# Attention over 32 heads: row maxima run 15 units ahead of the scores, per head instead of per group

## The reference

```python
q = x @ Wq
k = x @ Wk
v = x @ Wv
latent_kv = (k + v) @ W_down_kv
k_rec = latent_kv @ W_up_k
v_rec = latent_kv @ W_up_v
qh, kh, vh = (heads(q), heads(k_rec), heads(v_rec))
scale = 1.0 / (jnp.sqrt(jnp.float32(D_MODEL)) + 1e-08)
scores = jnp.einsum('bhqd,bhkd->bhqk', qh, kh) * scale
scores = jnp.clip(jnp.nan_to_num(scores, nan=-1000000000.0), -CLAMP, CLAMP)
decay = jnp.exp(-LAMBDA_DECAY * TIME_STEP * jnp.abs(idx[:, None] - idx[None, :]))
scores = scores * decay[None, None, :, :]
scores = jnp.clip(jnp.nan_to_num(scores, nan=-1000000000.0), -CLAMP, CLAMP)
attn = jax.nn.softmax(scores, axis=-1)
out = jnp.einsum('bhqk,bhkd->bhqd', attn, vh)
```

## Time and profile before

| | us |
|---|---|
| median of 3 runs | 954.49 |
| lowest, highest | 953.7, 958.48 |
| profiled execution | 959.48 |
| its span | 958.0 |
| attention in it (to the last output of the last group) | about 478 |
| mean granted clock of TensorE | 0.869 |

### The profile page before, as it was taken

One profiled execution on the slowest core, in us unless ns is written; L12 is line 12 of the kernel. 1 busy time (PEld: TensorE's weight loads), 2 busy tenths in 40 slices (PEclk: granted clock), 3 DMA queues, 4 the chain that ended last, 5 costly groups with the idle time before them and its releaser, 6 DMA issues. The chain is left out here.

```text
span 958.0 us, 25373 instructions
## 1 busy us (share of the span) xinstructions
PE 780.9 (82%) x10797; PEld 464.3 (48%) x10797; DVE 605.5 (63%) x1412; ACT 484.0 (51%) x974; POOL 220.0 (23%) x239
## 2 busy tenths in 40 slices
PE   6386999999999999999863958999998696026990
PEld 4012555555555555554442944666664354024770
DVE  3797769788878978780065232767676544762444
ACT  5522778787787778788831543434343222001222
POOL 3983121111121121212203724000000000005631
PEclk9555899999999999999965976999999797556995
DMA  5561215141314121000076126200000002201104
GB/s 190 147 228 61 66 27 76 26 77 30 71 35 72 33 68 38 4 3 5 2 233 175 49 61 227 72 1 1 2 1 1 0 1 67 69 0 39 40 26 143
DMA packets 45747, 59.08 MB, mean 62 GB/s; under 512 B 11924, under 2 KB 22877, under 8 KB 45632
## 3 DMA queue, kind: packets, MB, share of 16 engines
q1 hardware_dynamic: 42512, 51.47, 20.4%
q0 software_dynamic: 2304, 4.74, 1.9%
q10 hardware_dynamic: 816, 1.23, 0.4%
HBM read 42.09 MB, written 15.07 MB: 60 GB/s over the span
## 5 line engine op out<-in xcount | busy, mean ns | idle before, releaser
L800 DVE CUSTOM_DVE_ANT_0 junk<-row,rest 128x1024 bf16<-128x1024 f32 x256 | 307.8, 1223 | 60.4 <-PE row L421 47.1
L649 ACT ACTIVATE prob<-score 128x512 f32<-128x512 f32 x512 | 278.5, 612 | 85.7 <-PE score L421 81.0
L421 PE MATMUL score<-stack 75*32 75x128 bf16 (+3 forms) x3840 | 204.9, 300 | 5.7 <-DMA stack<-neg_rows 1.3
L514 PE MATMUL out_ps<-prob,v_aug 128*32 128x256 f32 x2048 | 153.9, 384 | 1.9 <-ACT prob L649 1.9
L421 PE MATMUL row<-stack 72*32 72x512 bf16 x1792 | 140.6, 389 | 2.1 <-DVE top L800 1.5
L421 PEld LDWEIGHTS score<-stack 75*32 75x32 bf16 x3840 | 91.9, 97 | 95.1 <-ACT prob L649 17.6
L736 POOL TENSOR_SCALAR_AFFINE_SELECT prob<-prob 128x512 f32<-128x512 f32 x64 | 40.6, 634 | 295.7 <-ACT prob L649 295.7
L514 PEld LDWEIGHTS out_ps<-prob,v_aug 128*32 128x32 f32 x2048 | 61.4, 111 | 38.6 <-ACT prob L649 3.3
L421 PEld LDWEIGHTS row<-stack 72*32 72x32 bf16 x1792 | 47.2, 98 | 35.4 <-issue 5.0
L1945 PE MATMUL outs<-vm_w,mixed 128*64 128x256 f32 x512 | 61.7, 381 | 1.8 <-issue 1.8
L1426 PE MATMUL up_ps<-rows_t,up_w 128*128 128x320 f32 (+1 forms) x192 | 60.0, 438 | 1.4 <-DVE rows_t L1638 1.2
(11 more groups left out here) (312 smaller groups left out, 1058.3 us busy)
## 6 DMA issues: line engine op xcount, KB each, us to landing
stack<-parts_dram SPq DMA_DIRECT2D x288, 64.0 KB
parts_dram<-prob SPq DMA_DIRECT2D x12, 256.0 KB, 3.2
parts_dram<-stack SPq DMA_DIRECT2D x12, 256.0 KB, 3.0
results<-x_tok SPq DMA_DIRECT2D x12, 256.0 KB, 3.6
up_w<-in_L_ffn_w_dram SPq DMA_DIRECT2D x1, 2048.0 KB, 9.6
rows<-x_tok SPq DMA_DIRECT2D x8, 256.0 KB, 3.7
y<-results SPq DMA_DIRECT2D x8, 256.0 KB, 4.2
up_w<-in_L_ffn_wg_dram SPq DMA_DIRECT2D x1, 2048.0 KB, 11.3
```

The lines of the kernel that those rows point to most:

```text
L421: last = pe.matmul(out[c:c + 32, :], keys[:, c:c + 32], queries, start=True, stop=True)
L514: last = pe.matmul(out_ps[at:at + 32, part * (S // 4):(part + 1) * (S // 4)], v_aug[g.third][:, tile, h, :], moving[:, 2 * part:2 * part + ...
L649: act.activation(prob[tile % 2][:, h, part * HALF:(part + 1) * HALF], score[n % NS][:, :], ACT.Exp).then_inc(exped, 1)
L800: dve.tensor_tensor_reduce(junk[:, n % 2, :], row[n % 2][:, :], rest[:, S - P - tile * P:2 * S - P - tile * P], 1.0, LOWEST, ALU.mult, ALU ...
```

## The change

What it does, piece by piece:

- **Units by head.** The groups of four are gone from the order. Attention is now 256 steps, one for each head m and key tile t (step = 8m + t). A step has two score units, a late unit at t = 3 and 7 (four diagonal blocks of one head), a row unit of step + LEAD (LEAD = 15), sometimes one extra slot (`slots_at`), and the products of key tile t-2. Row units, transposed maxima, turned outputs and the verdict share the two `row` buffers in one order (`slot_at`, `free_row`).
- **Start.** 15 wide row units run ahead of the first score, instead of 32.
- **Maxima.** They are split on GpSimd, per head, in four dependent operations on 8 columns (`split_top`), transposed by PE NEG_LAG = 2 slots after the head's last row unit, copied by DVE (`copy_neg`), stored by SP, 24 source rows into 3 rows of the stack (`store_neg`). The three keys are now -1 instead of 1 (`TWO_MINUS_ONES`), so nothing is negated.
- **Masks.** One affine select of 128 columns for each step, and one of 512 for each late unit.
- **Loads.** The stacks are now two, with four slots of two heads (a pair) each. The DRAM layout of the parts has the dimension ahead of the head, and one DMA (`load_block`) brings 24 partitions (three parts x 8 dimensions) of 2 heads, 96 KB: on side 0 the three query parts, on side 1 one key part three times. A pair and half takes 6, a pair 12 (`fill`), instead of 36 loads of 64 KB for four heads. SP issues `fill(pair + 3)` after the last score of the preceding pair (36 score units a pair), and behind it the stores of two heads' maxima.
- **Outputs.** A group's outputs are turned by 8 smaller transposes into a `row` buffer; the products of a head that opens a group are delayed so that the copy of the sums can pass.
- **Setup.** The key weights are folded first. The query weights are reordered by DVE. DVE splits both halves of batch 0, GpSimd half 0 of batch 1 in the setup and half 1 of it in the steps 0 to 10 of the pipeline (with ScalarE). ScalarE squares the four projections, and 32 one-column matmuls (`lengths`) ahead of the first wide row unit sum them into squared lengths.
- **Verdict.** The judging of the clamps is done in the last steps of attention, with no branch inside it; if it fails, the general routine does the attention afresh afterwards.

The core of the diff:

```diff
+def load_block(sp, dram, stack, pair, half, side, k, loaded):
+    at, h = k * NPART * HD, 2 * (pair % 2)
+    group = pair // 2
+    if side == 0:
+        rows = dram["parts"][0, half, :, group, :, h:h + 2, :]
+    else:
+        rows = dram["parts"][1, half, k, group, :, h:h + 2, :].unsqueeze(0).to_broadcast([NPART, HD, 2, S])
+    sp.dma_start(stack[at:at + NPART * HD, half, side, h:h + 2, :], rows).then_inc(loaded, 16)
+def load_pair(sp, dram, stack, pair, half, loaded):
+    for side in range(2):
+        for k in range(NPART):
+            load_block(sp, dram, stack, pair, half, side, k, loaded)
+LOADS = 2 * NPART
+LEAD = 15
+NEG_LAG = 2
+VERDICT_AT = 2
+OUT_AT = 4
 def attention(nc, mem, dram, io):
...
+        def leads_group(m):
+            return m > 0 and m % GH == 0
+        def weighs_at(step):
+            m, t = step // SB, step % SB
+            if t < 2:
+                return [("tile", m - 1, SB - 2 + t)] if m else []
+            if leads_group(m):
+                tiles = {4: (0, 1), 5: (2, 3), 6: (4,), 7: (5,)}.get(t, ())
+            else:
+                tiles = (t - 2,)
+            order = [("tile", m, tile) for tile in tiles] if m < NH else []
+            if t == 2 and m:
+                order.append(("late", m - 1, 1))
+            if t == SB - 1 and m < NH:
+                order.append(("late", m, 0))
+            return order
...
+        def slots_at(step):
+            n = step + LEAD
+            if n < NR:
+                yield "row", n
+            m, r = divmod(n - NEG_LAG, SB)
+            if r == SB - 1 and 0 <= m < NH:
+                yield "neg", m
+            if step >= GH * SB and step % (GH * SB) == OUT_AT:
+                yield "out", step // (GH * SB) - 1
+            if step in (STEPS - LEAD + VERDICT_AT, STEPS - LEAD + 2 * VERDICT_AT):
+                yield "verdict", (step - STEPS + LEAD) // VERDICT_AT - 1
+        LAST = STEPS + OUT_AT + 1
...
+            sp.wait_ge(rows_set, 1)
+            for k in range(NPART):
+                store_parts(sp, 0, 0, 0, k, kept[0][k])
+            store_parts(sp, 0, 0, 1, 0, kept[1][0])
+            for k in range(NPART):
+                sp.wait_ge(kept[0][k], 16)
+            for k in range(NPART):
+                load_block(sp, dram, stack[0], 0, 0, 0, k, stacks_in[0][0])
+            for k in range(1, NPART):
+                store_parts(sp, 0, 0, 1, k, kept[1][k])
+            for k in range(NPART):
+                sp.wait_ge(kept[1][k], 16)
+                load_block(sp, dram, stack[0], 0, 0, 1, k, stacks_in[0][0])
+            load_pair(sp, dram, stack[0], 1, 0, stacks_in[0][1])
+            for side in range(2):
+                for k in range(NPART):
+                    store_parts(sp, 0, 1, side, k, stored[0])
+            sp.wait_ge(stored[0], FILL * 16)
+            for pair in range(2):
+                load_pair(sp, dram, stack[0], pair, 1, stacks_in[1][pair])
+            def store_neg(m):
+                tile, h = of_head(m)
+                sp.wait_ge(row_done, slot_at["neg", m] + 1)
+                for half in range(2):
+                    sp.dma_start(tile[KR:KR + NPART, half, 0, h, :].rearrange("k (t c) -> k t c", c=P),
+                                 neg_rows[:, m % 2, :]).then_inc(neg_in[m % 2], 16)
+            def fill(pair):
+                for half in range(2):
+                    load_pair(sp, dram, stack[pair // 2 % 2], pair, half, stacks_in[half][pair % 4])
+            store_neg(0)
+            sp.wait_ge(rows_set, 2)
+            fill(2)
+            store_neg(1)
+            fill(3)
+            for k in range(FILL):
+                store_parts(sp, 1, 0, k // NPART, k % NPART, stored[1])
+            store_neg(2)
+            for pair in range(1, PAIRS):
+                if pair == 2:
+                    sp.wait_ge(late_part2, 4)
+                    for k in range(FILL):
+                        side, n = k // NPART, k % NPART
+                        if n == 0:
+                            sp.wait_ge(part[1][0], 3 + side)
+                        sp.dma_start(dram["parts"][side, 1, n, NG // B:NG, :, :, :].rearrange("g r h t -> (g r h) t"),
+                                     parts[1][1][:, side, n, :]).then_inc(stored[1], 16)
+                if pair == 5:
+                    sp.wait_ge(stored[1], 2 * FILL * 16)
+                if pair + 3 < PAIRS:
+                    sp.wait_ge(scored, 2 * UNITS * pair)
+                    fill(pair + 3)
+                for m in (2 * pair + 1, 2 * pair + 2):
+                    if m < NH:
+                        store_neg(m)
...
+            def lengths(b, side):
+                n = 2 * b + side
+                pe.wait_ge(squared, n + 1)
+                if n == 0:
+                    pe.wait_ge(v_copied, 2)
+                    pe.wait_ge(ones_in, 1)
+                for t in range(SB):
+                    at = side * NT + b * SB + t
+                    last = pe.matmul(bank[7][:, at:at + 1], squares[:, n % 3, t * P:(t + 1) * P], ones[:, :], start=True, stop=True)
+                last.then_inc(normed, 1)
+            for b in range(B):
+                for side in range(2):
+                    lengths(b, side)
             def by_columns(out, keys, queries):
...
+            def free_row(n):
+                if n >= 2:
+                    pe.wait_ge(row_done, n - 1)
+                return row[n % 2]
...
+            def turn_neg(m):
+                out = free_row(slot_at["neg", m])
+                pe.wait_ge(neg_chain, NEG_STEPS * (m + 1))
+                pe.transpose(out[0:NPART * SB, 0:P // 2].bitcast(BF16),
+                             neg_parts[:, m % 2, :, :], ident_b[:, :]).then_inc(row_ready, 1)
...
+            for step in range(LAST):
+                m, t = step // SB, step % SB
+                if step < STEPS:
+                    for part in range(2):
+                        score_unit(m, t, part)
+                    if t % 4 == 3:
+                        score_late(m, t // 4)
+                for kind, n in slots_at(step):
+                    if kind == "row":
+                        row_unit(n)
+                    elif kind == "neg":
+                        turn_neg(n)
+                    elif kind == "out":
+                        turn_out(n)
+                    elif n == 0:
+                        turn_lengths()
+                    else:
+                        turn_longest()
...
+            def split_top(m):
+                base = m * NEG_STEPS
+                values, pieces = top[:, m % 2, :], neg_parts[:, m % 2, :, :]
+                pool.wait_ge(row_done, slot_at["row", (m + 1) * SB - 1] + 1)
+                pool.tensor_copy(pieces[:, 0, :], values).then_inc(neg_chain, 1)
+                pool.wait_ge(neg_chain, base + 1)
+                pool.tensor_tensor(top_left[:, :], values, pieces[:, 0, :], ALU.subtract).then_inc(neg_chain, 1)
+                pool.wait_ge(neg_chain, base + 2)
+                pool.tensor_copy(pieces[:, 1, :], top_left[:, :]).then_inc(neg_chain, 1)
+                pool.wait_ge(neg_chain, base + 3)
+                pool.tensor_tensor(pieces[:, 2, :], top_left[:, :], pieces[:, 1, :], ALU.subtract).then_inc(neg_chain, 1)
...
+            for step in range(STEPS):
+                m, t = step // SB, step % SB
+                w = t // 4
+                at = t * P
+                pool.wait_ge(exped, unit(m, t, w) + 1)
+                pool.affine_select(out=prob[:, t, at:at + P], in_=prob[:, t, at:at + P], compare_op=ALU.is_ge, fill=0.0,
+                                   base=0, pattern=[[1, P]], channel_multiplier=-1).then_inc(masked, 1)
+                if t % 4 == 3:
+                    of = slice(w * HALF, (w + 1) * HALF)
+                    pool.wait_ge(exped, late_unit(m, w) + 1)
+                    pool.affine_select(out=prob_late[:, m % 2, of].rearrange("p (n c) -> p n c", c=P),
+                                       in_=prob_late[:, m % 2, of].rearrange("p (n c) -> p n c", c=P),
+                                       compare_op=ALU.is_gt, fill=0.0, base=0, pattern=[[0, 4], [-1, P]],
+                                       channel_multiplier=1).then_inc(mask_late, 1)
+                head, r = divmod(step + LEAD - 1, SB)
+                if r == SB - 1 and 0 < head < NH:
+                    split_top(head)
+                if step < 4:
+                    late_first_left(step)
+                elif 6 <= step < 10:
+                    late_second_left(step - 6)
+                elif step in (12, 20):
+                    set_values(1 + (step == 20))
+                if t == 0 and m % GH == 3 and m + 1 < NH:
+                    stage(m // GH + 1)
...
+            def copy_neg(m):
+                slot = slot_at["neg", m]
+                dve.wait_ge(row_ready, slot + 1)
+                if m >= 2:
+                    dve.wait_ge(neg_in[m % 2], m // 2 * 32)
```

(53 more changed lines are left out.)

844 lines of the change are left out of this document (336 added, 508 removed).

## The result

| | kernel before | changed kernel |
|---|---|---|
| median of 4 runs, us | 955.84 | 1045.81 |
| lowest to highest | 953.7 to 958.48 | 1041.99 to 1049.24 |
| profiled execution, and its span | 959.48, 958.0 | 1045.33, 1043.9 |

The ratio is 1.0951, 95% interval 1.092 to 1.0981: about 90 us slower. 1050 us was forecast, within 1000 to 1105.

The account below looks back on a forecast made before the run. TensorE was taken to bound the pipeline, with maxima delayed behind three-engine loads. Attention would end at 68+398+109 = 575 us against 478, +97, giving 1056 or 1051, stated as 1050 us, range 1000 to 1105.

Parts of the forecast that it names:

- Three engines: Stack loads: a leading dimension of 3 confines each to three DMA engines, 72 GB/s, 1.35 us a 96 KB block.
- Behind the fill: Pipeline: odd heads' maxima queue behind twelve blocks, so TensorE stands 7.3 or 5.7 us, mean 6.5, in pairs 3 to 12.
- S+19: Landing of head 2p+1's maxima, 19 us after pair p starts (time S); needed at S+11.7, or S+13.3 opening a group.
- The clock: TensorE after each wait for maxima: 2 us added for work at half clock, bounds 0 and 7.
- Their sum: Pipeline's waits with their half-clock work: 85 for pairs 3 to 12, 12, 5 and 7 for the others, 109 us.
- Arithmetic without waits: Attention from first score to end without any transfer wait: 398 us, with 1.45 us a unit with maxima.
- GpSimd's stall: TensorE waiting for GpSimd's split of the maxima: 0.2 us x 30 = 6 us (0 to 15).
- The shared banks: Row banks shared with transposes: late scores hide the wait in ordinary heads; group-opening heads pay about 1 us x 7.
- Setup: Before the pipeline: first row unit at 42 us (38 to 48), first score at 68, 20 before today's.
- The rest of the span: Everything after attention's end at 478 us: untouched by the change, should only move along.
- The range: Whole kernel, 1000 to 1105 us, from bounds on block time, clock and GpSimd.
- Rival (a): Loads spread over many engines, fill over before the maxima are ready: faster, 934 us (925 to 945); chance 0.17.

Follow-up runs that it names:

- the kernel with eight engines: Changed kernel with the 24 rows of each load ordered by dimension first, then part: 939.26 us, ratio 0.9783 to the kernel before.
- both mends: Changed kernel with load rows reordered by dimension first and each head's maxima issued ahead of six blocks: 939.3 us, ratio 0.9785 to the kernel before.
- the later transpose: NEG_LAG 3 instead of 2, in the changed kernel with reordered load rows and maxima issued ahead of blocks: 950.38 us, ratio 0.9836 to the kernel before.

## Why the prediction was right

- **Three engines.** Right: 0.19 to 0.20 while a fill runs, and reordering rows undoes it. The block was put at 1.35 us; 1.29 to 1.42 is measured. The row that it was concluded from, 0.24, is 3.8 of 16 engines, so the evidence was thinner than "near three" sounds.
- **Behind the fill.** Right in place. S+19 was forecast; the scores of pairs 3 to 12 come 18.3 to 19.0 us after SP starts the fill, but for that of head 15 with 20.5 (290.71 to 311.24), the longest. Over-sized in the wait itself: 5.3 us in the mean for these ten against 6.5, since the score was needed later, at S+12.9 (S+14.2 where a pair opens a group) instead of S+11.7 and S+13.3. Pair 1 was given 5 us and had no wait: SP issued its fill at 94.78, while TensorE still stood for head 2 until 102.04, and TensorE then ran at half clock. Pair 2 was given 12 for the stores of batch 1 ahead of its fill, and waited 4.5.
- **The clock.** Under-sized: 2 us a wait was taken, 46.3/12 = 3.9 is measured.
- **Their sum.** 108.1 us against 109 is closer than the terms are: without the 2 us of clock at each of 13 waits, 83 us of standing were forecast, and 61.8 more idle time is measured; 26 us of clock were forecast and 46.3 measured. That these two misses cancel is luck.
- **Arithmetic without waits.** 398 us was forecast from the first score to the end; the kernel with eight engines needs 389.7 between its first and last exponentials and some 4 to drain. A unit was put at 1.45 plus 0.12 for the transpose and 0.2 for GpSimd in a head, 11.92 a head; 11.85 is measured. GpSimd's stall was put at 6 us and is 6.8 (8.6 with both mends); its chain was put at 0.5 to 1.3 and takes 1.01.
- **The shared banks.** That late scores hide them is borne out by the later transpose, at 0.4 a head where they don't; the 1 us taken for heads that open a group was not measured by itself (such a head takes 13.2 against 11.85, turned output included; 1.6 was forecast).
- **Setup.** First row 42, measured 46.1: the 32 matmuls are two passes each and take 0.216 a pass at half clock, which was not priced. First score 68, measured 66.5. The miss of the first row did not count, as the first score hung on the transfers: 8 us less in front of the rows left it at 68.1.
- **The rest of the span.** It was to "only move along", and is 6.8 us shorter: 93 us at attention's end, 86 in the span. Of this 1.3 lies between the last exponential and the first `up_ps` matmul (34.8 before, 33.5 in the changed kernel), so in the end of attention; the other 5.5 lie in parts that the change leaves alone, and no run says why. The profiled execution of the kernel before was itself 5 us above its median.
- **The range.** Its lower end adds all three terms at their lower ends (1050-20-24-6 = 1000); the upper ends, added in the same way, give 1154 and not 1105. The measured time lies near the middle, so nothing hung on it.

Rival (a), loads on many engines, describes a kernel one edit away: 934 was worked out for it, and 939 is measured with eight engines.

## What to carry to other kernels

Look at the slowest dimension of both sides of every DMA; a 3 in front (parts, a broadcast) left three engines here, and swapping two dimensions of rows that may stand in any order gave eight. A small transfer that something waits for goes ahead of the bulk in its queue; a second queue let it be issued earlier, but it still stood 8 us beside the bulk (one run). A periodic wait of TensorE costs more than its length: the work at half clock behind it came to 0.75 of the idle time here (46.3 on 61.8), and to 1.4 of it with waits of 2.2 us (34.0 on 24.8), of which the shortest cost no clock at all.

## What was not expected of the hardware

- The issue time of a load did not go with its bytes: 0.74 us for 24 rows with 96 KB, 0.73 with 192 KB, against 0.34 for 8 rows with 32 KB (12.15 us for 36) and 0.35 with 64 KB (3.13 us for 9). Cutting a load of 24 rows in three costs 1.4 times the issue, not three times.
- One chip ran the same stage behind attention in 84 to 85 us, two others in 90 to 92, whatever the kernel; a difference of spans taken on two chips can be that.
